# A state-space layer with an FP4 feed-forward on one core: conv blocks and silu(z) through HBM, a lag of 20 blocks, and new queue orders

## The reference

```python
xz = x @ W_in;  x_proj, z = split(xz)                 # x: 8 x 2048 x 256, D_INNER 512
x_conv = silu(depthwise_conv(x_proj, 4 taps) + conv_b)
ssm = x_conv @ W_xproj                                # 33 columns: delta, B (16), C (16)
deltaB = softplus(ssm[..., 0])[..., None] * ssm[..., 1:17]
h_mean = einsum('bld,bln->bdn', x_conv, deltaB) / L   # a mean over the whole sequence
y = einsum('bdn,bln->bld', h_mean, ssm[..., 17:]) + D * x_conv
x = layernorm(x + (y * silu(z)) @ W_out)
# feed-forward: both operands of each product quantized to FP4 in blocks of 16
h = silu(fp4_linear(x, w_gate)) * fp4_linear(x, w_up) # 704 wide
out = layernorm(x + fp4_linear(h, w_down))
```

## Time and profile before

| | |
|---|---|
| Median of 3 runs | 2203.39 us (2200.66 to 2206.25) |
| The profiled execution | 2204.03 us, span 2202.1 us |
| TensorE matmuls busy | 1990.6 us, 90% of the span, 10532 instructions |
| Weight loads busy | 1583.8 us, 72% |
| VectorE busy | 1756.7 us, 80% |
| ScalarE busy | 1111.5 us, 50% |
| GpSimd busy | 1115.6 us, 51% |
| Granted TensorE clock, mean | 0.980 of full speed |
| DMA | 90.53 MB, mean 41 GB/s |

### The profile page before, as it was taken

How to read it: one execution, slowest core, us unless ns; L and a number is a source line. 1 busy time by engine, 2 the same in 40 slices (tenths; PEclk the granted TensorE clock), 3 DMA queues, 4 the chain that set the end, 5 groups by cost and what they waited for, 6 DMA issues and landing times.

```text
span 2202.1 us, 37847 instructions
## 1 busy us (share of the span) xinstructions
PE 1990.6 (90%) x10532; PEld 1583.8 (72%) x10532; DVE 1756.7 (80%) x3548; ACT 1111.5 (50%) x2100; POOL 1115.6 (51%) x1643
## 2 busy tenths in 40 slices
PE   1887899899999999899999999899999999877776
PEld 1655688688877888688877888688876888666665
DVE  6234788798978888789877888798887888788875
ACT  2665455555545555455544556455544555423332
POOL 2223455466545556455644555465554556445543
PEclk9999999999999999999999999999999999999998
DMA  2111111111111111111111111111111111000000
GB/s 79 50 56 43 34 49 44 44 43 45 49 41 34 44 48 45 36 49 49 41 38 41 44 44 48 38 49 44 39 41 39 49 45 35 29 20 25 20 20 15
DMA packets 77089, 90.53 MB, mean 41 GB/s; under 512 B 8881, under 2 KB 59953, under 8 KB 76849
## 3 DMA queue, kind: packets, MB, share of 16 engines
q1 hardware_dynamic: 76848, 87.73, 12.2%
HBM read 37.37 MB, written 16.78 MB: 25 GB/s over the span
## 4 chain that ended last, share of the span: by engine, by line
PE 76%; issue 5%; DVE 4%; ACT 3%; POOL 1%; ACTq 0%; DVEq 0%; POOLq 0%
PE pgu L489 23%; PE pd L489 14%; PE pd L537 9%; PE pa L489 6%; PE pb L489 6%; PE pc L571 4%; PE pc L519 4%; PE pe_ L631 2%; PE pa L559 2%; PE pc L496 2%; PE pe_ L548 1%; PE pd L638 1%; DVE hbuf L990 1%; DVE qsh L820 1%; PE pa L615 1%
## 5 line engine op out<-in xcount | busy, mean ns | idle before, releaser
L489 PE MATMUL pgu<-wgu_hi,xqT 128*128 128x512 f32 (+1 forms) x1536 | 427.7, 387 | 0.9 <-issue 0.9
L489 PE MATMUL pd<-wd_hi,hqT 128*128 128x256 f32 (+1 forms) x1536 | 334.5, 299 | 18.7 <-DVE r L1012 15.5
L489 PEld LDWEIGHTS pgu<-wgu_hi,xqT 128*128 128x128 f32 x1536 | 279.8, 190 | 75.8 <-issue 27.6
L537 PE MATMUL pd<-wout,g 128*128 128x256 f32 x1024 | 259.9, 398 | 49.6 <-DVE hqT L980 35.2
L489 PEld LDWEIGHTS pd<-wd_hi,hqT 128*128 128x128 f32 (+1 forms) x1536 | 255.8, 190 | 57.4 <-issue 23.8
L946 DVE SCALAR_TENSOR_TENSOR acc<-xps,cw,acc 128x512 f32<-128x512 f32 x256 | 248.7, 972 | 24.4 <-POOL acc L429 23.7
L418 POOL TENSOR_SCALAR rs<-mv 128x1 f32<-128x1 f32 x128 | 61.6, 481 | 396.4 <-DVE mv L1027 228.8
L537 PEld LDWEIGHTS pd<-wout,g 128*128 128x128 f32 x1024 | 191.5, 195 | 79.7 <-issue 56.0
L741 ACT ACTIVATE hqT<-pe_ 128x512 fp32r<-128x512 f32 x128 | 76.2, 595 | 335.3 <-PE pe_ L631 335.3
L402 POOL TENSOR_TENSOR xv<-xnq,qsx 128x256 f32<-128x256 bf16 x128 | 79.5, 621 | 300.1 <-DVE xnq L839 300.1
L489 PE MATMUL pgu<-wgu_lo,xqT 128*128 128x512 f32 (+1 forms) x768 | 228.3, 379 | 0.0
(11 more groups left out here) (132 smaller groups left out, 4669.2 us busy)
## 6 DMA issues: line engine op xcount, KB each, us to landing
xcr<-xcs SPq DMA_DIRECT2D x128, 256.0 KB, 2.3
xin<-in_L_attn_x_dram SPq DMA_DIRECT2D x32, 512.0 KB, 3.9
xres<-in_L_attn_x_dram SPq DMA_DIRECT2D x128, 128.0 KB, 2.1
out_dram<-outb SPq DMA_DIRECT2D x128, 128.0 KB, 1.7
szr<-in_L_attn_W_in_dram SPq DMA_DIRECT2D x1, 1024.0 KB, 7.4
szr<-in_L_ffn_w_down_dram SPq DMA_DIRECT2D x1, 704.0 KB, 8.6
szr<-in_L_ffn_w_gate_dram SPq DMA_DIRECT2D x1, 640.0 KB, 4.5
szr<-in_L_ffn_w_up_dram SPq DMA_DIRECT2D x1, 640.0 KB, 5.7
```

Source lines behind the costliest of these rows:

```text
L489: mm = pe.matmul(bank, lhsT, rhs, start=(m == 0), stop=(m == len(pairs) - 1))
L537: mm = pe.matmul(pd[:, 0:DM], g[:, (s + 1) % 2, c, j * P:(j + 1) * P], wout[:, c, :], start=(c == 0), stop=(c == NB - 1))
```

## The change

- `walk` has a lag of `SPS + 1` = 5 super steps (20 blocks): `i = g_ - LAG`. `late_y`, `tail_here` and `ring_place` go; all super steps have one form. The partial state is in the step `j == 1`, the transposes of C and the mean state in `j == 3`.
- The rings `xcr` and `szr` go. SP saves each conv block to `xc_hbm` and each silu(z) (from `szs`, two buffers) to `sz_hbm`, and loads block `w + 1` of both into `xl` and `zl` (two buffers each).
- The scaled codes of h have a buffer of their own, `hq`; `hbuf` is smaller. The last two transposes of h go to bank `pb` in place of `pd`.
- TensorE's step is now: gate and up, product x, transposes of h, y product, output projection, (partial state), state projection, transposes of conv and of x, product z, down projection. In `j == 1` the state projection and the transposes of conv come behind product z.
- VectorE's step begins with r2 and its statistics for block `tz` (they were the last, for `td`), then `q_add` and `q_take` of h for `td`, quantization of x up to the divide, both taps, `q_add` and `q_take` of x, product and absmax of h, the two low halves of `hqT`, and only then the skip addition, scale and inverse of h, r1, divide of h, statistics, state addition, low half of x.
- ScalarE's step is: abs of x, silu of the conv block, silu of the gate, `xps` and `acc`, copies to `hqT`, tap 0, output, abs of h, copy of the conv transposes, copy of x, silu of z, r1.
- GpSimd's step is: product of the codes of h, layer norm 2, `hist`, product of the codes of x, addition of tap 0, gate product, layer norm 1.
- The scratch space of the weight preparation is a tile of its own, since the rings that it used are gone.

```diff
+    LAG = SPS + 1
+    xc_hbm = nc.dram_tensor("xc_hbm", [NT, P, ST], F32)
+    sz_hbm = nc.dram_tensor("sz_hbm", [NT, P, ST], F32)
...
-        szr = sb("szr", [P, NB, SPS, ST])
-        xcr = sb("xcr", [P, NB, SPS, ST])
+        xl = sb("xl", [P, 2, ST])
+        zl = sb("zl", [P, 2, ST])
+        szs = sb("szs", [P, 2, ST])
...
-        hbuf = sb("hbuf", [P, FF + (FC + 1) * P])
+        hbuf = sb("hbuf", [P, 2 * FF])
+        hq = sb("hq", [P, (FC + 1) * P])
...
+        def stages(g, j):
+            u = 4 * g + j
+            w = u - 4 * LAG
+            return u, u - 1, w, w - 4, w - 5, w - 6, w - 7, w - 8
```

SP's step (the whole body but for the load of `xin`):

```diff
                     if exists(to + 1):
                         at_least(q, r_done, to)
                         q.dma_start(xres[:, (j + 1) % 2, :], xtile[to + 1])\
                             .then_inc(xres_landed[(j + 1) % 2], 16)
+                    if exists(w + 1):
+                        n, half = (j + 1) % 2, 16 * (2 * i + (j + 1) // 2 + 1)
+                        wait_apart(q, (xc_saved[n], half), (sz_saved[n], half), (g_ready, w))
+                        q.dma_start(xl[:, n, :], xc_hbm[w + 1]).then_inc(xl_landed[n], 16)
+                        q.dma_start(zl[:, n, :], sz_hbm[w + 1]).then_inc(zl_landed[n], 16)
...
-                        wait_apart(q, (xc_ready, v + 1), (yd_done, w))
-                        q.dma_start(xcr[:, jb, sb_, :], xcs[:, jb % 2, :]).then_inc(xc_saved[jb % 2], 16)
+                        q.wait_ge(xc_ready, v + 1)
+                        q.dma_start(xc_hbm[v], xcs[:, (j + 1) % 2, :]).then_inc(xc_saved[(j + 1) % 2], 16)
                     if exists(tz):
                         q.wait_ge(out_ready, tz + 1)
                         q.dma_start(of[tz], outb[:, j % 2, :]).then_inc(out_saved[j % 2], 16)
+                    if exists(u):
+                        q.wait_ge(z_ready, u + 1)
+                        q.dma_start(sz_hbm[u], szs[:, j % 2, :]).then_inc(sz_saved[j % 2], 16)
```

TensorE's step and the waits in it that the prediction speaks of:

```diff
+                    if j == 0 and p1:
+                        transposed_input(g_, u, v)
+                    if exists(tg):
+                        gate_and_up(tg)
+                    if p1:
+                        x_product(j, g_, u, v)
+                    if exists(td):
+                        transposed_h(td, u)
+                    if p2:
+                        y_product(j, s, b, g_, v, w)
+                    if exists(to):
+                        output_projection(j, s, i, tz)
+                    if j == 1 and tail:
+                        partial_state(g_, w)              # waits: dB_ready, xct_copied, yd_done w + 1
+                    if j != 1 and exists(v):
+                        state_projection(j, jb, g_, v, w) # waits: xc_ready, yd_done w + 1, ssm_added
+                        transposed_conv(jb, u, v)
+                    if exists(tx):
+                        transposed_x(td, tx)
+                    if p1:
+                        z_product(j, u, td)               # waits: z_ready, hqT_hi and hqT_lo 2 * td + 2
+                    if j == 1 and exists(v):
+                        state_projection(j, jb, g_, v, w)
+                        transposed_conv(jb, u, v)
+                    if j == 3 and tail:
+                        transposed_c(g_, v)
+                    if exists(td):
+                        down_projection(to, td)           # waits: hqT_hi, hqT_lo, r_done to + 1
```

The head of VectorE's step, and the skip addition that now stands in the middle:

```diff
+                    if exists(tz):
+                        dve.wait_ge(dn_pe, tz + 1)
+                        at_least(dve, out_ready, tz)
+                        dve.tensor_tensor(r2[:, :], pd[:, 0:DM], r1[:, j, :], ALU.add).then_inc(r2_done, 1)
...
+                    if p2:
+                        dve.wait_ge(y_pe, w + 1)
+                        dve.wait_ge(xl_landed[j % 2], 16 * (2 * i + j // 2 + 1))
+                        at_least(dve, o_pe, 4 * i - 4)
+                        dve.scalar_tensor_tensor(g[:, second(s) % 2, j, :], xl[:, j % 2, :], dsk[:, j:j + 1], pc[:, :],
+                                                 ALU.mult, ALU.add).then_inc(yd_done, 1)
```

More of the change, by code:

```diff
@@ L511, in partial_state @@
[L511 to L517 removed]
+                for k in range(KM):
+                    for t in range(TPS):
+                        mm = pe.transpose((pa, pb)[k][:, t * P:(t + 1) * P],
+                                          xin[:, t, k * P:(k + 1) * P], ident[:, :])
+                    mm.then_inc(xt_pe, 1)
@@ new lines, in x_product, with transposed_h @@
+            def x_product(j, g_, u, v):
+                if j == 0:
+                    pe.wait_ge(xt_l, 2 * g_ + 2)
+                at_least(pe, xct_copied, v)
+                at_least(pe, xp_copied, u)
+                projection(pa[:, :], slice(j * P, (j + 1) * P)).then_inc(xp_pe, 1)
+            def transposed_h(td, u):
+                pe.wait_ge(hprod_done, td + 1)
+                pe.wait_ge(z_ready, capped(u, NT))
+                for n in range(FC + 1):
+                    bank = pe_[:, n * P:(n + 1) * P] if n < 4 else pb[:, (n - 4) * P:(n - 3) * P]
+                    mm = pe.transpose(bank, hq[:, n * P:(n + 1) * P], ident[:, :])
+                    if n in (3, FC):
+                        mm.then_inc(hq_pe, 1)
@@ new lines, in y_product, with output_projection @@
+            def y_product(j, s, b, g_, v, w):
+                wait_apart(pe, (h_ready, b - 1 if s == 0 else b), (ct_ready, g_ - LAG + 1), (yd_done, w),
+                           (ssm_added, capped(v, NT)))
+                pe.matmul(pc[:, :], hcat[:, j * P:(j + 1) * P], ctr[:, second(s), :], start=True, stop=True)\
+                    .then_inc(y_pe, 1)
+            def output_projection(j, s, i, tz):
+                pe.wait_ge(g_ready, 4 * i)
+                at_least(pe, r2_done, capped(tz + 1, NT))
+                for c in range(NB):
+                    mm = pe.matmul(pd[:, 0:DM], g[:, (second(s) + 1) % 2, c, j * P:(j + 1) * P],
+                                   wout[:, c, :], start=(c == 0), stop=(c == NB - 1))
+                mm.then_inc(o_pe, 1)
@@ L936, in body @@
                     jb = (j - 1) % NB
[L937 removed]
+                    h, h_big = hbuf[:, FF:2 * FF], hbuf[:, 0:FF]
                     def tap(k):
```

582 lines of the change are left out of this document (226 added, 356 removed).

## The result

The changed kernel takes **2825.84 us** (median of 4 runs, 2825.05 to 2834.8), the kernel before 2202.06 (2200.66 to 2206.25): ratio 1.284, 95% interval 1.281 to 1.287. I had said 2703 us, 2460 to 2790, slower. The sign and the mechanism came out, the size did not: the time lies above the range.

The account below looks back on a forecast made before the run. TensorE bounds the kernel before; after, a ring between VectorE and TensorE was to. Start 54, first half 149, filling 100, 25 super steps of 80.0 (2000), drain 398 and 2 around the span: 2703 us, range 2460 to 2790.

Parts of the forecast that it names:

- The ring: Plain step: VectorE's r2 to skip addition, 11.2 us, then TensorE's state projection to down projection, 5.4, plus 0.3: 16.9 us.
- hold-up that I took at 0.5: VectorE's part of the ring: GpSimd's scaling of codes delays the divide of x, 0.5 us, between 0 and two of 0.74.
- The clock's price per stall: Behind TensorE's stall of about 3.2 us in each plain step, the lower clock adds 1.6 us: 18.5 instead of 16.9.
- The super step without the clock: A full super step, four plain steps and TensorE's other work, takes 73.6 us without the clock's part, 80.0 with it.
- The signs: Full super steps: idle of about 3 us before the state projection, TensorE's busy share under 0.8, granted clock near 0.91.
- First half: Five super steps with only the first half at 29.8 us each, 149 us, set by the conv chain as before.
- Filling and drain: Filling 100 us against 94 before; drain 28 steps of 14.2 us, 398 us, against 24 steps of 12.84.
- HBM trips at nothing: Three new 256 KB DMAs per step cost nothing; loads land some 7 us before the skip addition reads them.
- `hq` and the bank: Own buffer for scaled codes and bank `pb` remove the output projection's wait for hqT, 1.72 us per drain step.
- The boundary, "at most 70 us": Where a batch element ends, the longer lag drops the special order and can win back at most 70 us over six places.
- the clock stays up: Rival: the ring as said, but its repeated stalls do not lower TensorE's clock: 2509 us, chance 0.25.
- heavier contention: Rival: GpSimd holds VectorE up twice or more per step, 0.9 us more in the ring: 2806 us, chance 0.08.

Follow-up runs that it names:

- the run with z first: Changed kernel with product z right behind the state projection in three steps of four, transposes of conv and x after z: 2771.7 us (1.260).
- the other kernel: Changed kernel with the old queue orders and bank, C transposes one super step later: 2220.7 us; with all loops written out too, 2188.7 us.

## Why the prediction was right or wrong

- **The ring**: right. VectorE's part 11.47 us against 11.2, TensorE's 5.55 at full clock against 5.4 and a hand-over, 100 stalls released by the skip addition, r2 waiting for the down projection. Moving the skip addition removed the stalls (2490 us). The hold-up that I took at 0.5 shows at another instruction than I named and is larger: the scale of x takes 1.22 us in all 100 full steps, where before has 0.16, and ends with GpSimd's product of the codes beside it (627.33 to 628.72). That this product is its cause was not tested. The wait for ScalarE is 0.55 in this step.
- **The clock's price per stall**: the step that failed. I took 1.6 us from a window of 6 us behind one stall and let it stand for a hundred. Measured: 2.9 us in the turn shown, 2.7 on average by the run with 22 matmuls. The 1.1 to 1.3 us more, 4 x 25 times, are 110 to 130 of the 132 us. The 1.6 itself was rightly read: it is the price of a low stretch of 3.4 us, and the run with z first has it again. What I had wrong is how long the clock stays low in the ring, 6.8 us behind 83 of the 100 stalls. Why 6.8 and not 3.4 stays open. The range failed with it: its ends were "no price" and "1.6 us", and nothing beyond the one row. The rule of the Trainium skill that I had as a rival ("TensorE: Matmul & The Clock Gate", Part 1, a penalty under 1%) gave 2509 us; the trace disagrees, since the run with 22 matmuls, at 2581 us, shows the clock to be worth at least 245 of 2826 us here. I had also written that the trace of the kernel before agrees with it; it doesn't, for its mean granted clock of 0.980 is 2% below full speed.
- **The super step without the clock**: 73.6 us said; 74.7 with the clock back.
- **The signs**: TensorE's busy share stayed at 0.84 in the full super steps, not under 0.8 as I had written, and the clock was 0.85, not 0.91. Both follow from the longer low stretches, in which TensorE is busy for longer with the same work.
- **First half**: 29.8 us per super step said, 158.9 / 5 = 31.8 measured. The kernel with the old orders and C moved, which has the trips to HBM too, takes 30.7 (153.4 us for five, from 54.09 to 207.47), so about half of the excess comes with the new orders. What sets the rest, the trips among the possible causes, was not tested.
- **Filling and drain**: 100 and 398 said, 95.3 and 399.8 measured. The drain's terms fit less than their sum: steps of 13.5 us where the clock is full and 17.0 where it is not.
- **HBM trips at nothing**: right, 2.8 and 3.0 us per load:

```profile
xl<-xc_hbm SPq DMA_DIRECT2D x128, 256.0 KB, 2.8
zl<-sz_hbm SPq DMA_DIRECT2D x128, 256.0 KB, 3.0
```

  The skip addition never waits for them. The cover is greater than I said: what is issued at the head of a step is read in the next one.
- **`hq` and the bank**: the output projection has no wait any more, as said. I had counted it as harmless at worst; the other bank alone, in the drain of before, lost 58 us. `hq` alone was not run.
- **The boundary, "at most 70 us"**: right as a bound, wrong as a description. 25 us were turns of the loops, and with the longer lag 5.3 to 6.0 us of each boundary went only when the state's copy moved too. In the changed kernel the ring hides all of it: its super steps around a turn take 87.7 and 83.0, that is 2 x 85.3.
- **The rivals**: "the clock stays up" and "heavier contention" were not it; the latter's time (2806) is near the measured one for a wrong reason. No load came late.

## What to carry to other kernels

When a price is read off a single event and is to be multiplied by a hundred, look up every such event that the trace has: here one stall was followed by 3.4 us of low clock and another of nearly the same length by 6.8. Let the range reach to the dearest of them. Before an instruction is moved behind others on its queue, follow who needs its result in the same pass: one skip addition, moved, was worth 335 us. A wait that is removed from the middle of a ring comes back elsewhere in it, and a place where it joins another can be dearer than where it was.

## What the runs showed of the hardware that I had not expected

- The granted clock's low stretches come in about three lengths, 3.4, 6.8 and 10 us, in kernels whose stalls differ by under 1 us. How often each length comes changed with the stall (in the full super steps 72 of 91 were short with 6 matmuls, 17 of 100 with none) and with the work behind it (z first). What decides between them stays open, since two stalls alike to 0.01 us were followed by one of each, and the drain with 43.5 of 50 us busy ran at 0.93, that with 38.8 of 50 at 1.00.
- Useless matmuls paid: 22 of 128x256 in each full step, 88 more instructions on TensorE per super step, 245 us less in all.
- A turn of the loops, with a body of four super steps, cost 5 to 6.4 us (25 us over 5 turns in before, 32 in the other kernel), and nothing was gained by writing out TensorE's loop alone. The trace calls these stalls "issue"; it gives the same name to a stall whose cause was a semaphore of VectorE's. So "issue" is a place to look in the code, not a cause.
